# An index copy moved ahead of the wait for logits in a four-layer graph network kernel, and one set of row stores left out

## The reference, cut to what matters

```python
N, E, D, L = (5000, 80000, 64, 4)          # 165000 directed edges with self loops
def _genconv(x, src, dst, ea, W1, b1, lg, lb, W2, b2, t):
    m = relu(x[src] + ea) + EPS
    logits = m * t
    mx = segment_max(logits, dst); e = exp(logits - mx[dst])
    denom = segment_sum(e, dst);   alpha = e / denom[dst]
    agg = segment_sum(m * alpha, dst)
    h = relu(_ln((agg + x) @ W1 + b1, lg, lb))
    return h @ W2 + b2
...
x = _genconv(x, ...)                        # layer 0
for i in range(1, L):                       # layers 1 to 3
    h = relu(_ln(x, normG[i], normB[i]))
    x = x + _genconv(h, ...)
return relu(_ln(x, normG[0], normB[0])) @ linW + linb
```

## Time and profile before

| | |
|---|---|
| median of 3 runs | 11827.7 us (11806.76 to 11829.9) |
| the profiled execution | 11828.1 us, its span 11826.3 us |
| TensorE, busy | 5802.2 us (49%) |
| VectorE, busy | 6551.7 us (55%) |
| ScalarE, busy | 3327.1 us (28%) |
| GpSimd, busy | 6522.0 us (55%) |

### The profile page before, as it was taken

How to read it: one execution, slowest core, us unless ns; L and a number is a source line. 1 busy time by engine, 2 the same in 40 slices (tenths; PEclk the granted TensorE clock), 3 DMA queues, 4 the chain that set the end, 5 groups by cost and what they waited for, 6 DMA issues and landing times. The chain is left out here.

```text
span 11826.3 us, 107787 instructions
## 1 busy us (share of the span) xinstructions
PE 5802.2 (49%) x31762; PEld 4077.1 (34%) x31762; DVE 6551.7 (55%) x8055; ACT 3327.1 (28%) x4948; POOL 6522.0 (55%) x6157
## 2 busy tenths in 40 slices
PE   2333333343444444444444444444444447888887
PEld 2222222232333333333333333333333334444443
DVE  5666666664444444544444445444444457998897
ACT  1333333342333333333333333333223232111110
POOL 5455455535444444454544444544444446888887
PEclk6666666666666666666666666666666668999998
DMA  5344344333333333333333333333333334555555
GB/s 155 125 137 138 123 140 132 130 109 103 118 117 117 117 117 117 102 97 116 119 118 118 117 118 106 95 117 118 117 117 117 117 112 94 99 97 99 96 94 86
DMA packets 840467, 1354.58 MB, mean 115 GB/s; under 512 B 499934, under 2 KB 556476, under 8 KB 838730
## 3 DMA queue, kind: packets, MB, share of 16 engines
q1 hardware_dynamic: 523832, 1135.94, 27.5%
q0 software_dynamic: 312640, 214.30, 12.9%
q10 hardware_dynamic: 3916, 3.40, 0.1%
HBM read 806.66 MB, written 546.46 MB: 114 GB/s over the span
## 5 line engine op out<-in xcount | busy, mean ns | idle before, releaser
L826 POOL DMA_INDIRECT xg<-h_tab,idx x4656 | 4461.7, 958 | 4370.0 <-DVE idx L1159 2909.3
L917 PE MATMUL turn<-hb,hot 125*128 125x192 bf16 x12480 | 1872.5, 295 | 3018.0 <-issue 2977.7
L917 PEld LDWEIGHTS turn<-hb,hot 125*128 125x128 fp8e4 x12480 | 1310.6, 114 | 3571.7 <-issue 3536.0
L1159 DVE COPY idx<-idx_full 128x24 int32 x208 | 36.6, 176 | 3526.7 <-ACT zl L1035 3526.7
L933 PE MATMUL turn<-ident,sums 128*128 128x128 f32 x5184 | 1073.7, 375 | 1533.8 <-ACT st_all L1050 1140.4
L1524 POOL DMA_INDIRECT acc<-vm,tgt x1026 | 1602.9, 1562 | 341.2 <-issue 288.1
L933 PEld LDWEIGHTS turn<-ident,sums 128*128 128x128 f32 x5184 | 878.0, 222 | 1676.3 <-ACT st_all L1050 1243.6
L1066 ACT ACTIVATE hx<-turn 128x384 bf16<-128x384 f32 x156 | 76.4, 490 | 3600.9 <-PE turn L917 3553.1
L1050 ACT ACTIVATE st_all<-turn 128x512 f32<-128x512 f32 (+1 forms) x1344 | 752.3, 577 | 698.7 <-PE turn L933 321.0
L1166 DVE TENSOR_TENSOR_SCAN rx<-rp,carry,zl 128x1536 f32<-128x1536 bf16 (+1 forms) x224 | 739.9, 3303 | 360.1 <-ACT zl L1035 343.1
L1597 PE MATMUL zl<-spreadz,lo_hot 128*128 128x512 f32 x1620 | 765.5, 609 | 95.2 <-DVE spreadz L1773 95.2
(11 more groups left out here) (277 smaller groups left out, 7413.2 us busy)
## 6 DMA issues: line engine op xcount, KB each, us to landing
sums<-st_all SPq DMA_DIRECT2D x208, 1536.0 KB
hot<-hot_tab SPq DMA_DIRECT2D x312, 625.0 KB
ea<-feat SPq DMA_DIRECT2D x158, 768.0 KB
srcB<-src_flat SPq DMA_DIRECT2D x108, 768.0 KB
rp<-run_pen SPq DMA_DIRECT2D x210, 384.2 KB
xg<-h_tab,idx POOLq DMA_INDIRECT x4656
hot_tab<-hot SPq DMA_DIRECT2D x104, 625.0 KB
run_head<-zeros SPq DMA_DIRECT2D x216, 192.0 KB
```

The costliest lines, as they stand in the source:

```text
L826: g_.indirect_dma_start(xg[b][:, k, h, :], None, h_tab[:, :], bass.IndirectOffsetOnAxis(ap=idx[b][:, h, k:k + 1] if small is None else idx ...
L917: ins = pe.matmul(picked[:, :, n % 2, :], hot[n][0:PN, t_, :], hb[0:PN, t_, :, :], start=t_ == 0, stop=t_ == NT - 1, skip_group_check=True)
```

## The change

In layers 1 to 3 VectorE no longer copies the index columns of window w+2 behind its wait for the logits of window w. It waits for TensorE's three groups of `forward` (`z_ps`, the last reader of `xg[b]`, and so the proof that the gathers have read `idx[b]`), copies, and then waits for the logits. Layer 0 keeps its copy behind the maxima. Besides, SP no longer stores `h_cur` to `h_tab` after the last layer, and waits for ScalarE's last chunk itself instead of for the landing of these stores.

```diff
-                        for k in range(NCH):
+                        for k in range(NCH if l + 1 < L else 0):
                             sp.wait_ge(h_ok, NCH * l + k + 1)
                             store_nodes(k)
...
-                    sp.wait_ge(tab_out, 16 * NCH * L + 16)
+                    sp.wait_ge(tab_out, 16 * NCH * (L - 1) + 16)
+                    sp.wait_ge(h_ok, NCH * L)
...
                     def window(g, w, i, l, b, width=W):
                         link = Chain(v, dve_step, g * STEPS)
+                        if width == W and l:
+                            v.wait_ge(z_ps, NG * (g + 1) + Z0)
+                            next_lists(w + 2, b)
                         v.wait_ge(l_ok, g + 1 + L0)
-                        if width == W and l:
-                            next_lists(w + 2, b)
```

## The result

The changed kernel takes 11288.8 us, median of 4 runs (11280.3 to 11310.4); the kernel before, in 4 runs, 11825.7 us. The ratio is 0.9552, 95% interval 0.9535 to 0.9569: 537 us less. The profiled execution took 11284.7 us, with a span of 11283.0.

What follows compares the result with a forecast made beforehand. Gathers of layers 1 to 3 were taken to wait on the index copy, in one loop with TensorE's slowed select. 11828.1 - 559 (147 windows x 3.8) - 1.3 = 11267.8, so 11270 us, range 11170 to 11700.

Steps and rivals of the forecast that it cites:

- crawl: TensorE's select slowed while GpSimd issues gathers: 17 matmuls in 24.4 us, pace back 3.9 us after the last gather.
- The stock: About 120 TensorE instructions issued at full pace from the first gather until the crawl; a count, not a time.
- Select again gets 46 at full pace: After the change TensorE still does 46 of select's matmuls at full pace before the crawl.
- 0.5 us given back: The crawl ends 4.4 us sooner, so 3 select matmuls remain for afterwards, 0.17 us each: 0.5 us.
- The ring: One window of layers 1 to 3, through select, transposes, copy, gathers and pace back: 37.8 us against 41.6.
- The stores: Dropping the last h_cur stores after layer 3 takes 1.3 us off, between 0 and 2.
- The smaller stock: Only 34 select matmuls run at pace, a window takes 40.1 us, 250 us saved: 11575 us; chance 0.17.
- The handshakes under gathers: Back's last four groups drag on under gathers, select runs behind them, windows about 45 us: 12270 us; chance 0.16.
- Nothing gained: Select's lost time belongs to its program place; windows keep 42 us, only the stores go: 11826 us; chance 0.05.
- Gathers' wait for the copy: In the changed profile GpSimd's wait for the index copy falls from 14.8 to about 10.4 us a window.
- release by the transposes: In the changed profile VectorE's index copy is released by TensorE's transposes, no longer by ScalarE.
- back under 5 us: In the changed profile back's four groups on TensorE still take under 5 us.

Runs made afterwards that it cites:

- lists_ahead: Changed kernel with the index copy of layers 1 to 3 waiting only until the earlier gathers have landed; 11208.0 us, ratio 0.9476 to the kernel before.
- one_column_2: Changed kernel with one hot column instead of two in layers 1 to 3 and lists copied ahead as in lists_ahead; 10856.7 us, ratio 0.9189.
- the fewer gathers: Changed kernel with 10 of 22 gathers left out in the full windows of layers 1 to 3; 9306.2 us in one run.

## Why the prediction was right, and where it was off

Predicted 11270, measured 11288.8. Medians over 132 windows of layers 1 to 3 (windows 5 to 48 of each), counted in the traces. The first column runs to the start of the last matmul at pace, the last one is the distance between the starts of successive selects:

| | first gather to crawl | TensorE instructions in it | of select at pace | left when the pace returns | window |
|---|---|---|---|---|---|
| before | 7.1 us | 116 | 47 | 19 | 42.2 us |
| after | 11.7 us | 111 | 39 | 31 | 38.5 us |
| lists_ahead | 14.6 us | 115 | 32 | 41 | 38.1 us |
| one_column_2 | 12.5 us | 126 | 32 of 40 | 1 | 34.8 us |

**The stock is a count: right.** The time to the crawl doubles, the instructions stay at 111 to 126. These are medians; in the changed kernel single windows lie between 98 and 123. The Trainium skill, NOTIFIC — the notification-queue block, section 7.1, has an inner queue that fills and then holds its producers back; the runs agree so far that the stall comes by filling and not by time, and none shows that it is that block. The set without the crawl, with the same instructions and gathers, says that something outside the kernel takes part. Every run here lists a span and a granted clock, which come from records taken as it ran; none ran without them. Whether the crawl would be there without the recording is a rival that no run tests. For the fetching of instructions as the cause there is little: in the changed kernel's page two queues of that kind carry 36 and 43 packets in all, fewer than the 147 windows that crawl.

```profile
q8 instruction: 36, 0.59, 0.0%
q14 instruction: 43, 0.35, 0.0%
```

**"Select again gets 46 at full pace": wrong, 39.** The failed step is the sum of the stock. (In the window read, 92 and 32 instructions are 124 and not 120, and the time is 6.8 us, 6039.27 - 6032.43, and not 7.1; neither matters to the choice.) I counted 32 instructions of back behind the old first gather. But in the earlier trace rows those 16 transposes start at 6031.65 and the gather at 6032.43: only 116 - 2 x 47 = 22 lay behind it. After the change it is 111 - 2 x 39 = 33. Of the 8 matmuls lost, 5.5 are these 11 instructions; the other 2.5 are the stock, 5 smaller, which I can't explain.

**"0.5 us given back": too small, about 1.3.** 31 matmuls are left instead of 18, and the crawl did 10. They take 4.4 us (median, to the end of the last), not 3.1. They cost less each (0.14 us) than the 0.17 taken, which kept the miss small: the granted clock is at 0.50 (1.2 GHz) when the crawl ends, and can rise within a longer tail. Of these two stretches the first holds the last 18 matmuls of one tail, 0.10 us each, the second all 30 of the next, 0.17 each (the last three columns are the granted clock, the DMA share and GB/s):

```profile
5979.60:5981.60 2.00, 2.00 (x23) 1.97 (x22) 0.00 (x0) 0.07 (x1) 0.00 (x0) 0.89 0.32 118
6015.40:6020.40 5.00, 4.98 (x31) 4.73 (x32) 0.00 (x0) 0.00 (x0) 0.00 (x0) 0.50 0.21 80
```

**The other terms held.** The copy 0.17 us behind the transposes (0.3 taken), the first gather 1.15 behind it (1.17), 27.4 of gathers, the pace back after 3.6 (3.9). The ring is 4.4 + 1.95 + 0.2 + 1.15 + 27.4 + 3.6 = 38.7 us, 38.5 as measured, against 37.8 predicted. A window lost 3.7 us by the medians (42.2 to 38.5), close to the 3.8 forecast, only because the ring before was 42.2 and not the 41.6 of the window that I took: two errors of 0.6 to 0.7 us cancel, and that is luck. By the sums over 50 windows it lost 3.4 us in the first execution and 3.7 in the second. The stores gave 1.5 for 1.3.

**The rivals.** The smaller stock came true in part: layer 3 has windows with 33 to 36 at pace and 35 to 38 left, at 40 us, in turn with others at 38. The handshakes under gathers stayed away in layers 1 to 3: back's 16 transposes take 3.72 us, before 3.73. "Nothing gained" is refuted by the fewer gathers where the crawl is, and is what happens where it isn't: I gave that 0.05 for the wrong reason, a place in the program, and never asked whether the stall would be there in the next execution.

**Signs.** Gathers' wait for the copy 455.4/41 = 11.1 us (10.4 said, 14.8 before); release by the transposes, yes; copies 38.5 apart (38); 39 at pace (43 to 50, missed), 31 left (20, missed); back under 5 us, yes.

## What to carry to other kernels

An engine that loses time to "issue" while another one issues indirect DMAs may be held by them: look where that block begins and ends, count the stalled engine's instructions from its start, and move the block, or instructions out of it, with that count in hand. Starting the block earlier pays only as far as the work that it then covers fits in the count; fewer instructions paid more here (one hot column less, some 340 us against lists_ahead by the ratios) than the still earlier start (81 us). Idle time put down to "issue" can be a plain wait: look at what the first instruction behind it waits for. And run the kernel before beside every candidate: the same pair of layouts changed sign, 0.92 against 1.01, between two sets.

## What the hardware did that I had not expected

The kernel before takes 11812 to 11830 us in three sets and 8774 in another, with gathers of 958 ns in both. Where it takes 11800, TensorE issues 111 to 126 instructions from the first gather of a block on, then one in about 0.8 to 1.3 us, and is back at pace 3.6 to 4.1 us after the last; a sixteenth of the bytes changes none of it. Where it takes 8774, no such gap exists. What sets the one or the other, whether the recording of the runs has a part in it, and whether plain DMAs issued by GpSimd would do the same, stays open.
